# Half sums and differences of keys, and value products in two bursts: a change to a four-layer Trainium2 kernel

## The chip, the cores and the metric

One core of a Trainium2 chip runs the whole program. The metric is the device time of one execution in microseconds. The engines are TensorE (PE; PEld is its weight load), VectorE (DVE), ScalarE (ACT), GpSimd (POOL) and SyncE (SP), which here only issues DMAs.

## The reference, cut to what matters

Four transformer layers are applied in turn to x of 4 x 1024 x 128, each an attention and a feed-forward part, each added to x. The change lies in the attention of the first two layers, which have 16 heads of 8 features. Layer 1 is causal:

```python
scores = jnp.einsum('bthd,bshd->bhts', q, k) / math.sqrt(dk)
scores = jnp.where(causal_mask, -inf, scores)
attn = jax.nn.softmax(scores, axis=-1)
out = jnp.einsum('bhts,bshd->bthd', attn, v)
```

Layer 2 has no mask, has a bias on q, k and v, and subtracts the maximum of each row of scores in the open:

```python
scores = jnp.einsum('bhqd,bhkd->bhqk', q, k) * SCALE
scores = scores - jnp.max(scores, axis=-1, keepdims=True)
attn = jnp.exp(scores)
attn = attn / jnp.maximum(jnp.sum(attn, axis=-1, keepdims=True), 1e-12)
ctx = jnp.einsum('bhqk,bhkd->bhqd', attn, v)
```

## The kernel before

`project` normalises the rows, turns them and forms q, k and v in eight chunks of 512 rows. An item is q or k of one chunk: one fp32 product of 128x512 into `item_ps`, which is then split into three bf16 parts. ScalarE writes the first part (`high`), VectorE the remainder, ScalarE the second part (`middle`), GpSimd the third, and SP stores the three to DRAM. Its tensors are called p0 in layer 1 and p1 in layer 2; a page of the profile leaves such numbers out.

`narrow_attention` is used by both layers (tensors a0 and a1). A unit is one batch and four heads, 16 units in all. The bf16 parts of q and k lie as 6 pairs of 8 rows, 48 rows for a head; two heads share the 128 rows of an operand, one in each half, so that two products can lie in different rows of TensorE. Work of a unit comes in two kinds:

- Slots, for the row maxima. A slot is a product of 128 queries with 512 keys of one head, into one of three PSUM banks `slot_ps` (`a_slot`, L1181). VectorE reduces it to one column of `part_max` (L1344; in layer 1 with a mask added, L1340). There are 64 in a unit of layer 2: 4 heads, 8 tiles of 128 queries, 2 halves of the keys (`kh`). Layer 1 has 48, of 128 to 512 columns. A further slot takes the turn of the maxima (`max_turn`), and two that of the outputs (`o_turn`), which need the same banks. A bank is free again when `slot_done` says so.
- Steps, for the output: 16 of 128 keys by 512 queries (12 in layer 1, from 128 to 512 queries wide). In each, for e in 0, 1: two score products of two heads, transposed, with minus the maximum added through three further rows (L1203; masks L1210), and one exponential of ScalarE over both (L1321). Then the value products of the step before: four fp32 products of 32 columns each, for the four heads, into one bank `o_ps` (`values`, L1223). The last head's columns carry the sum of the exponentials along.

The slots run ahead: those for step n + 5 (layer 1: n + 6) are issued during step n (`ahead`), four a step in layer 2, so unit 0's and the first 20 of unit 1's come before the first step. TensorE's order is written out by hand: for each e a quarter of the step's slots, the two scores, another quarter; after both, the values. At the end of a half of the queries ScalarE copies `o_ps` out (`copy_out`, L1308), and the next half's first value product waits for that.

Of the kernel before, what the change touches and what calls it, by code (L numbers as in the profile page):

```python
# [7 lines left out]
BF16 = mybir.dt.bfloat16  # L8
# [109 lines left out]
def project(nc, name, src, mv, rstd, wq, wk, wv, qs, ks, vs, ident, load_early, gain=None, qk_bias=None, v_bias=None, fresh=None):  # L118


    NB, ITEMS = 4, 2
    groups = ((0,), (1,), (2, 3), (4, 5), (6, 7))
    with ExitStack() as ctx:
# [6 lines left out]
        def sem(n):  # L130
            return nc.alloc_semaphore(f"{name}_{n}")

        w_qk = [sb(f"w_qk{i}", [P, P]) for i in range(ITEMS)]
# [7 lines left out]
        gain_sb, bias_sb, vb_sb = sb("gain_sb", [P, 2]), sb("bias_sb", [P, ITEMS]), sb("vb_sb", [P, P])  # L141
# [5 lines left out]
                             "v_ready", "v_done"))  # L147
        stats_done, mv_done, std_done, root_step = (sem(n) for n in ("stats_done", "mv_done", "std_done", "root_step"))
        stored = [sem(f"stored{i}") for i in range(2 * NB)]
        v_stored = [sem(f"v_stored{i}") for i in range(4)]  # L150
        n_loads = 3 + sum(a is not None for a in (gain, qk_bias, v_bias))
# [3 lines left out]
        def _(sp):  # L155
# [4 lines left out]
            if qk_bias is not None:  # L160
                sp.dma_start(bias_sb[:], qk_bias).then_inc(loaded, 16)
            if v_bias is not None:
                sp.dma_start(vb_sb[:], v_bias.to_broadcast([P, P])).then_inc(loaded, 16)
            for c in range(CHUNKS):
                b, half = c // 2, c % 2
                for i in range(ITEMS):
                    n = c * ITEMS + i
                    sp.wait_ge(lo_done, n + 1)
                    sp.dma_start((qs, ks)[i][b, :, :, half * CH:(half + 1) * CH].rearrange("k f t -> f k t"),
                                 parts[n % (2 * NB)][:]).then_inc(stored[n % (2 * NB)], 16)  # L170
# [3 lines left out]
                if c == 3:  # L174
                    for i in range(4):
                        sp.wait_ge(stored[i], 16)
# [4 lines left out]
            for i in range(2 * NB):  # L181
                sp.wait_ge(stored[i], 16 * (CHUNKS * ITEMS // (2 * NB)))
# [4 lines left out]
        def _(te):  # L187
# [14 lines left out]
            for c in range(CHUNKS):  # L202
                te.wait_ge(xT_done, c + 1)
                for i in range(ITEMS):
                    n = c * ITEMS + i
                    if n >= NB:
                        te.wait_ge(rem_done, n - NB + 1)
                    nc.tensor.matmul(item_ps[n % NB][:], w_qk[i][:], xnT[c % 4][:], start=True, stop=True).then_inc(item_ready, 1)
# [10 lines left out]
        def _(act):  # L219
            def take(c):  # L220

                act.wait_ge(xT_ready, c + 1)
                if c >= 4:
                    act.wait_ge(v_ready, c - 3)
# [6 lines left out]
            def high(n):  # L231

                act.wait_ge(item_ready, n + 1)
                if n >= 2 * NB:
                    act.wait_ge(stored[n % (2 * NB)], n // (2 * NB) * 16)
                if qk_bias is None:
                    nc.scalar.activation(parts[n % (2 * NB)][:, 0, :], item_ps[n % NB][:], ACT.Copy).then_inc(hi_done, 1)
                else:
                    nc.scalar.activation(parts[n % (2 * NB)][:, 0, :], item_ps[n % NB][:], ACT.Identity,
# [2996 lines left out]
```

## Time and profile before

| | |
|---|---|
| median of 3 runs | 3596.66 us (3596.16 to 3596.76) |
| profiled execution | 3575.11 us, its span 3573.2 us |
| TensorE busy | 2981.4 us (83%) |
| VectorE busy | 2616.7 us (73%) |
| ScalarE busy | 2150.4 us (60%) |
| mean granted TensorE clock | 0.924 |

The busy shares are means over all stages. The steps of layer 1's attention run from about 111 to 553 us, those of layer 2's from 940 to 1594 us, with the projection of layer 2 before them, from about 838 us.

### The profile page before, as it was taken

How to read it: one execution, taken by the hardware profiler on the slowest of the kernel's cores; microseconds unless marked ns; L12 is line 12 of the kernel's file. 1: busy time of each engine (PE TensorE's matmuls, PEld its weight loads, DVE VectorE, ACT ScalarE, POOL GpSimd, SP SyncE). 2: the span in 40 equal slices, each digit the busy share in tenths (PEclk: the TensorE clock that was granted, in tenths of full speed). 3: DMA queues.
4: the chain of work that ended last, by engine and by line, in shares of the span. 5: the costliest groups of instructions: out<-in, count | busy, mean ns of one | idle time of the engine just before them, and what ended most of it. 6: DMA issues, size and time to landing. Idle time of an engine off the chain costs nothing. (4 is left out here: it accounts for less than half of the span.)

```text
span 3573.2 us, 51682 instructions
## 1 busy us (share of the span) xinstructions
PE 2981.4 (83%) x18320; PEld 1203.9 (34%) x18320; DVE 2616.7 (73%) x6042; ACT 2150.4 (60%) x2740; POOL 451.6 (13%) x633
## 2 busy tenths in 40 slices
PE   5999997896999999985799998967469988889836
PEld 2333333443122222223355555545322222222214
DVE  6999973666999999946566666640868888888821
ACT  2566673323377777773355555522369999899822
POOL 2000001333000000000000000014220011102023
PEclk7899998997799999997899999978779999999968
DMA  4443202343211111000000000011362222221102
GB/s 146 58 106 62 33 13 48 64 80 112 30 27 27 22 22 22 12 3 3 31 1 1 1 7 7 1 54 50 106 140 33 33 33 39 27 30 23 53 24 74
DMA packets 172975, 148.27 MB, mean 41 GB/s; under 512 B 79672, under 2 KB 130632, under 8 KB 172720
## 3 DMA queue, kind: packets, MB, share of 16 engines
q1 hardware_dynamic: 168624, 137.21, 19.2%
q0 software_dynamic: 4096, 7.78, 0.7%
q8 instruction: 145, 2.38, 0.3%
q14 instruction: 110, 0.90, 0.1%
HBM read 95.13 MB, written 49.68 MB: 41 GB/s over the span
## 5 line engine op out<-in xcount | busy, mean ns | idle before, releaser
L1321 ACT ACTIVATE a_probs<-a_scores 128x1024 f32<-128x1024 f32 (+3 forms) x896 | 791.5, 932 | 374.1 <-PE a_scores L1203 233.9
L1344 DVE TENSOR_REDUCE a_part_max<-a_slot_ps 128x1 f32<-128x512 f32 x1280 | 798.6, 684 | 30.9 <-PE a_slot_ps L1181 29.6
L2341 DVE TENSOR_TENSOR a_probs<-a_logit_ps,a_gate 128x1024 f32<-128x1024 f32 x512 | 602.4, 1219 | 98.8 <-ACT a_gate L2200 97.5
L1181 PE MATMUL a_slot_ps<-a_k_op,a_q_op 48*128 48x512 bf16 (+3 forms) x1792 | 579.1, 380 | 95.6 <-DMA a_mask_wide<-in_mask_wide 17.9
L2205 ACT ACTIVATE a_probs<-a_probs 128x2048 f32<-128x2048 f32 x256 | 488.1, 1907 | 7.7 <-DVE a_probs L2341 7.6
L1203 PE MATMUL a_scores<-a_q_op,a_k_op 51*128 51x512 bf16 (+3 forms) x1792 | 452.4, 361 | 7.1 <-ACT a_probs L1321 6.1
L1223 PE MATMUL a_o_ps<-a_probs,a_v_op 128*32 128x512 f32 (+3 forms) x3584 | 437.9, 561 | 1.2 <-ACT a_o_sb L1308 0.6
L1181 PEld LDWEIGHTS a_slot_ps<-a_k_op,a_q_op 48*128 48x128 bf16 x1792 | 150.2, 94 | 697.5 <-DVE a_part_max L1344 469.2
L2106 PE MATMUL a_logit_ps<-space 96*128 96x512 bf16 x1024 | 303.3, 387 | 71.2 <-DVE a_probs L2341 62.4
L2200 ACT ACTIVATE a_gate<-a_diff_ps 128x1024 f32<-128x1024 f32 x256 | 261.6, 1022 | 55.2 <-PE a_diff_ps L2106 47.5
L2119 PE MATMUL a_o_ps<-a_probs,a_v_op 128*32 128x512 f32 x2048 | 274.0, 607 | 7.0 <-DVE a_o_sb L2334 3.1
L1340 DVE CUSTOM_DVE_ANT_0 a_slot_ps<-a_slot_ps,a_mask_wide 128x128 f32<-128x128 f32 (+3 forms) x512 | 237.0, 516 | 5.1 <-PE a_slot_ps L1181 4.1
L757 ACT ACTIVATE a_turned_sb<-a_turn_ps 128x512 f32<-128x512 f32 x192 | 93.6, 488 | 208.0 <-PE a_turn_ps L632 207.8
L747 ACT ACTIVATE space<-space,a_lows 128x128 f32<-128x128 f32 (+7 forms) x256 | 195.2, 767 | 4.0 <-DVE a_lows L841 4.0
L632 PE MATMUL a_turn_ps<-ident_sb,space 128*128 128x128 f32 x1152 | 167.1, 277 | 22.7 <-DVE a_turned_sb L852 18.0
L852 DVE COPY a_turned_sb<-a_turn_ps 128x512 f32<-128x512 f32 x192 | 106.6, 555 | 95.6 <-PE a_turn_ps L632 95.1
L2106 PE MATMUL a_diff_ps<-space 96*128 96x512 bf16 x512 | 157.1, 389 | 15.1 <-DMA a_v_op<-scratch_v 15.1
L841 DVE CUSTOM_DVE_ANT_0 space<-a_score_ps,a_mask 128x512 f32<-128x512 f32 (+3 forms) x256 | 138.7, 587 | 37.3 <-PE a_score_ps L619 37.2
L2106 PEld LDWEIGHTS a_logit_ps<-space 96*128 96x128 bf16 x1024 | 77.0, 98 | 263.9 <-DVE a_probs L2341 219.4
L632 PEld LDWEIGHTS a_turn_ps<-ident_sb,space 128*128 128x128 f32 x1152 | 132.6, 141 | 70.1 <-issue 32.1
L619 PE MATMUL a_score_ps<-a_kT,a_qT 64*128 64x512 f32 (+3 forms) x768 | 152.3, 516 | 1.1 <-DVE a_lows L841 1.0
L646 PE MATMUL a_o_ps<-a_turned_sb,a_v 128*64 128x512 f32 (+3 forms) x768 | 149.9, 512 | 0.0
(400 smaller groups left out, 3758.3 us busy)
## 6 DMA issues: line engine op xcount, KB each, us to landing
e_coef<-coef_dram SPq DMA_DIRECT2D x16, 1024.0 KB, 9.9
a_q_op<-scratch_q SPq DMA_DIRECT2D x384, 32.0 KB
a_k_op<-scratch_k SPq DMA_DIRECT2D x384, 32.0 KB
scratch_q<-p_parts SPq DMA_DIRECT2D x24, 384.0 KB, 3.4
scratch_k<-p_parts SPq DMA_DIRECT2D x24, 384.0 KB, 3.4
space<-scratch_k SPq DMA_DIRECT2D x192, 32.0 KB
space<-scratch_g SPq DMA_DIRECT2D x192, 32.0 KB
space<-scratch_q SPq DMA_DIRECT2D x192, 32.0 KB
```

The costliest lines, as they stand in the source:

```text
L632: mm = nc.tensor.transpose(turn_ps[j][:, t * P:(t + 1) * P], rows_of(u, h, t)[0][:, j, kb * P:(kb + 1) * P], ident[:])
L1181: nc.tensor.matmul(out[:, 0:width], q_op[g][r0:r0 + MAX_ROW, e, qt * P:(qt + 1) * P], k_op[g][r0:r0 + MAX_ROW, e, kh * CH:kh * CH + width] ...
L1203: return nc.tensor.matmul(scores[e][:, jj, off:CH], k_op[g][r0:r1, e, kb * P:(kb + 1) * P], q_op[g][r0:r1, e, hq * CH + off:(hq + 1) * CH] ...
L1223: mm = nc.tensor.matmul(o_ps[32 * j:32 * (j + 1), off:CH], v_op[g][:, kb, 32 * j:32 * (j + 1)], probs[(u * S + n) % NB][:, j, off:CH], sta ...
L1321: nc.scalar.activation(probs[gs % NB][:, 2 * e:2 * e + 2, off:CH], scores[e][:, :, off:CH], ACT.Exp, scale=scale).then_inc(probs_done, 1)
L1340: nc.vector.tensor_tensor_reduce(out=slot[:, 0:w], in0=slot[:, 0:w], in1=mask_wide[:, CH - w:CH], scale=1.0, scalar=-3e38, op0=ALU.add, op ...
L1344: nc.vector.tensor_reduce(part_max[u % 2][:, kh, col:col + 1], slot[:, 0:w], axis=AX.X, op=ALU.max).then_inc(slot_done, 1)
L2106: mm = nc.tensor.matmul(out[:, j, :], ops[g][0][:, j, kb * P:(kb + 1) * P], q[:, j, hq * CH:(hq + 1) * CH], start=True, stop=True)
L2119: mm = nc.tensor.matmul(o_ps[c0:c0 + 32, :], v_op[g][:, kb, j * 32:(j + 1) * 32], probs[gs % 4][:, m, j, :], start=kb == 0, stop=kb == KB - 1)
L2200: nc.scalar.activation(gate[gs % 2][:], diff_ps[:], ACT.Tanh).then_inc(gate_done, 1)
L2205: nc.scalar.activation(tile[:], tile[:], ACT.Exp).then_inc(exp_done, 1)
L2341: nc.vector.tensor_tensor(probs[gs % 4][:, m, :, :], logit_ps[m][:], gate[gs % 2][:], op) \
```

## The change

In layer 2 only, the maximum over both halves of the keys is found for a quarter of the row tiles (those with an odd head of a pair and an odd query tile) by max(a, b) = (a + b) / 2 + |a - b| / 2. `project` forms a third kind of item, "h", once per batch: half sums and half differences of the two halves' keys, from weights that GpSimd halves (`w_half`), for one head of each pair. They go to `scratch_halves`, and SP loads them into `k_halves`. A slot with the differences (`apart`) goes to ScalarE, which writes its absolute value to `sizes`; VectorE skips it. The slot with the sums goes to VectorE, which adds `sizes` and takes the maximum in one instruction. The order of slots in a unit changes, and banks are freed by either of two semaphores. In both layers the value products of a step are issued in two bursts: after the slots and scores of e = 0 those of heads 0 and 1, after those of e = 1 those of heads 2 and 3.

```diff
@@ project, TensorE
+                    else:
+                        te.wait_ge(halved, 4)
+                        nc.tensor.matmul(item_ps[n % NB][:], w_half[0][:], xnT[(c - 1) % 4][:], start=True, stop=False)
+                        nc.tensor.matmul(item_ps[n % NB][:], w_half[1][:], xnT[c % 4][:], start=False, stop=True) \
+                            .then_inc(item_ready, 1)
...
@@ project, ScalarE
-                    act.wait_ge(v_ready, c - 3)
+                    act.wait_ge(v_ready, c - 2)
...
@@ project, GpSimd
+                for i, column, factor in ((0, 0, 0.5), (0, 1, 0.5), (1, 0, 0.5), (1, 1, -0.5)):
+                    nc.gpsimd.tensor_scalar(w_half[i][:].rearrange("p (g i e r) -> p g i e r", g=GROUPS, i=2, e=2)[:, :, column], odd,
+                                            factor, None, ALU.mult).then_inc(halved, 1)
...
@@ NarrowShape
+    EIGHT = ((0, 0, 0), (1, 0, 0), (0, 0, 1), (1, 1, 0), (0, 1, 0), (1, 0, 1), (0, 1, 1), (1, 1, 1))
...
+            self.slots = [(2 * e + jj, qt + odd, kh) for e in range(2) for qt in range(0, KB, 2) for jj, odd, kh in self.EIGHT]
...
+    def in_pair(self, s):
+        j, qt, kh = self.slots[s]
+        return not self.causal and j % 2 == 1 and qt % 2 == 1
+    def apart(self, s):
+        return self.in_pair(s) and self.slots[s][2] == 0
...
@@ NarrowOperands.load_qk, SP
+            if self.halves is not None:
+                src = self.halves[b, kp].rearrange("(g x r) t -> g r x t", g=GROUPS, r=8)
+                r0 = HALF_ROWS + n * 8
+                sp.dma_start(self.k_halves[g][r0:r0 + 8, :, :, :].rearrange("r i e t -> r (i e) t"), src[g]).then_inc(self.qk_loaded[g], 16)
...
@@ narrow_attention, TensorE
-                    te.wait_ge(slot_done, n - BANKS + 1)
+                    apart, count = shape.released[n - BANKS]
+                    te.wait_ge(size_done if apart else slot_done, count)
...
+                keys = k_op[g][r0:r0 + MAX_ROW, e, kh * CH:kh * CH + width]
+                if shape.in_pair(s):
+                    keys = operands.k_halves[g][r0:r0 + MAX_ROW, 1 - kh, e, :]
...
-            def values(u, n):
+            def values(u, n, e):
...
-                te.wait_ge(probs_done, (u * S + n + 1) * 2)
-                if n == 0:
+                te.wait_ge(probs_done, (u * S + n) * 2 + e + 1)
+                if n == 0 and e == 0:
                     te.wait_ge(v_spread, u + 1)
-                if kb == 0 and u * 2 + hq > 0:
+                if kb == 0 and e == 0 and u * 2 + hq > 0:
                     te.wait_ge(o_copied, u * 2 + hq)
-                for j in range(H):
+                for j in (2 * e, 2 * e + 1):
...
                         for v, s in todo[cut[2 * e + 1]:cut[2 * e + 2]]:
                             a_slot(v, s)
-                    if n > 0:
-                        values(u, n - 1)
-                    elif u > 0:
-                        values(u - 1, S - 1)
+                        if n > 0:
+                            values(u, n - 1, e)
+                        elif u > 0:
+                            values(u - 1, S - 1, e)
...
@@ narrow_attention, ScalarE
+            def slot_sizes(todo):
+                for u, s in todo:
+                    n = shape.place["slot", u, s]
+                    apart, count = shape.released[n]
+                    if apart:
+                        act.wait_ge(slot_ready, n + 1)
+                        if count > 2:
+                            act.wait_ge(slot_done, shape.released[shape.place["slot", *pairs[count - 3]]][1])
+                        nc.scalar.activation(sizes[(count - 1) % 2][:], slot_ps[n % BANKS][:], ACT.Abs).then_inc(size_done, 1)
...
                     for e in range(2):
+                        slot_sizes(todo[cut[2 * e]:cut[2 * e + 1]])
                         act.wait_ge(scores_ready, gs * 2 + e + 1)
...
                                              ACT.Exp, scale=scale).then_inc(probs_done, 1)
+                        slot_sizes(todo[cut[2 * e + 1]:cut[2 * e + 2]])
...
@@ narrow_attention, VectorE
+                if shape.apart(s):
+                    return
                 dve.wait_ge(slot_ready, n + 1)
+                if shape.in_pair(s):
+                    count = pairs.index((u, s)) + 1
+                    dve.wait_ge(size_done, count)
+                    nc.vector.tensor_tensor_reduce(out=slot[:], in0=slot[:], in1=sizes[(count - 1) % 2][:], scale=1.0,
+                                                   scalar=-3e38, op0=ALU.add, op1=ALU.max,
+                                                   accum_out=part_max[u % 2][:, kh, col:col + 1]).then_inc(slot_done, 1)
+                    return
```

On TensorE, from one step's value products to the next in the middle of layer 2's attention, the order of before is this (a row is line, operation, output and inputs, output's shape and the number in a row):

```order
L1223 MATMUL a1_o_ps<-a1_probs1,a1_v_op0 32x512 x4
L1181 MATMUL a1_slot_ps2<-a1_k_op2,a1_q_op2 128x512
L1203 MATMUL a1_scores0<-a1_q_op0,a1_k_op0 128x512 x2
L1181 MATMUL a1_slot_ps0<-a1_k_op2,a1_q_op2 128x512
L1181 MATMUL a1_slot_ps1<-a1_k_op2,a1_q_op2 128x512
L1203 MATMUL a1_scores1<-a1_q_op0,a1_k_op0 128x512 x2
L1181 MATMUL a1_slot_ps2<-a1_k_op2,a1_q_op2 128x512
L1223 MATMUL a1_o_ps<-a1_probs2,a1_v_op0 32x512 x4
```

The changed kernel has there:

```order
L1282 MATMUL a1_o_ps<-a1_probs3,a1_v_op1 32x512 x2
L1240 MATMUL a1_slot_ps0<-a1_k_op3,a1_q_op3 128x512
L1262 MATMUL a1_scores1<-a1_q_op2,a1_k_op2 128x512 x2
L1240 MATMUL a1_slot_ps1<-a1_k_halves3,a1_q_op3 128x512
L1282 MATMUL a1_o_ps<-a1_probs3,a1_v_op1 32x512 x2
L1240 MATMUL a1_slot_ps2<-a1_k_op3,a1_q_op3 128x512
L1262 MATMUL a1_scores0<-a1_q_op2,a1_k_op2 128x512 x2
L1240 MATMUL a1_slot_ps0<-a1_k_op3,a1_q_op3 128x512
L1282 MATMUL a1_o_ps<-a1_probs0,a1_v_op2 32x512 x2
```

The four value products of a step stand as two and two, with two slots and two scores ahead of each pair; the two slots that stood next to each other are parted by a pair.

On ScalarE, steps of the same stage before:

```order
L1321 ACTIVATE a1_probs0<-a1_scores1 128x1024
L1321 ACTIVATE a1_probs1<-a1_scores0 128x1024
L1321 ACTIVATE a1_probs1<-a1_scores1 128x1024
L1321 ACTIVATE a1_probs2<-a1_scores0 128x1024
L1321 ACTIVATE a1_probs2<-a1_scores1 128x1024
```

and in the changed kernel:

```order
L1398 ACTIVATE a1_probs0<-a1_scores0 128x1024
L1398 ACTIVATE a1_probs0<-a1_scores1 128x1024
L1398 ACTIVATE a1_probs1<-a1_scores0 128x1024
L1398 ACTIVATE a1_probs1<-a1_scores1 128x1024
L1380 ACTIVATE a1_sizes1<-a1_slot_ps1 128x512
L1398 ACTIVATE a1_probs2<-a1_scores0 128x1024
```

After every fourth exponential an absolute value of a difference slot has come in.

## Rows read from the trace of the kernel before

**Rows 1.** Busy time by stretch: attention of layer 1, attention of layer 2.

```profile
core 0: us, PE busy (x) PEld busy (x) DVE busy (x) ACT busy (x) POOL busy (x), PEclk, DMA share, GB/s
...
111.00:553.00 442.00, 412.32 (x4131) 162.13 (x4131) 374.71 (x1240) 303.88 (x412) 29.28 (x75) 1.00 0.29 54
940.00:1594.00 654.00, 620.67 (x4129) 133.52 (x4127) 605.98 (x1058) 508.77 (x541) 29.27 (x75) 1.00 0.14 20
...
```

**Rows 2.** Timeline of VectorE, start of attention in layer 2.

```profile
start us, us, engine line op out<-in xcount [idle before <-releaser]
...
885.17 38.36 DVE L1344 TENSOR_REDUCE a_part_max<-a_slot_ps 128x1 f32<-128x512 f32 x64 [14.56 <-PE a_slot_ps L1181]
...
```

**Rows 3.** Line of the row maxima: count, ns min/median/max, first and last start.

```profile
L1350 DVE TENSOR_TENSOR a_row_max<-a_part_max x4: 191/192/193, 207.8 to 293.2; 128x32 f32<-128x32 f32 x4
L1350 DVE TENSOR_TENSOR a_row_max<-a_part_max x4: 191/191/191, 1216.7 to 1342.5; 128x32 f32<-128x32 f32 x4
```

**Rows 4.** Timeline of TensorE, one step of attention in layer 2.

```profile
...
1226.34 1.07 PE L1223 MATMUL a_o_ps<-a_probs,a_v_op 128*32 128x512 f32 x8
1227.34 0.39 PE L1181 MATMUL a_slot_ps<-a_k_op,a_q_op 48*128 48x512 bf16 x1
1227.34 0.60 PE L1203 MATMUL a_scores<-a_q_op,a_k_op 51*128 51x512 bf16 x2
1227.57 0.64 PE L1181 MATMUL a_slot_ps<-a_k_op,a_q_op 48*128 48x512 bf16 x2
1228.51 0.39 PE L1181 MATMUL a_slot_ps<-a_k_op,a_q_op 48*128 48x512 bf16 x1
1228.82 1.06 PE L1223 MATMUL a_o_ps<-a_probs,a_v_op 128*32 128x512 f32 x8
...
```

**Rows 5.** Timeline of TensorE, attention in layer 1.

```profile
...
283.73 0.33 PE L1210 MATMUL a_scores<-a_mask_b,a_ident 64*128 64x128 bf16 x4
284.33 0.23 PE L1181 MATMUL a_slot_ps<-a_k_op,a_q_op 48*128 48x128 bf16 x1 [0.27 <-DVE a_part_max L1344]
284.48 0.85 PE L1223 MATMUL a_o_ps<-a_probs,a_v_op 128*32 128x384 f32 x8
285.26 0.66 PE L1195 MATMUL a_slot_ps<-ident_sb,a_o_sb 128*128 128x128 f32 x4
285.85 0.39 PE L1181 MATMUL a_slot_ps<-a_k_op,a_q_op 48*128 48x512 bf16 x1
...
```

**Rows 6.** Timeline of TensorE, attention of layer 3.

```profile
...
1900.48 1.94 PE L646 MATMUL a_o_ps<-a_turned_sb,a_v 128*64 128x512 f32 x8
1902.35 1.12 PE L666 MATMUL a_spare_ps<-a_xnT,a_w_q 128*128 128x512 f32 x2
```

**Rows 7.** Groups by shape, attention of layer 2: busy, mean ns, idle before.

```profile
...
L1344 DVE TENSOR_REDUCE a_part_max<-a_slot_ps 128x1 f32<-128x512 f32 x935 | 580.5, 683 | 1.9 <-PE a_slot_ps L1181 1.0
...
L1181 PEld LDWEIGHTS a_slot_ps<-a_k_op,a_q_op 48*128 48x128 bf16 x932 | 70.5, 93 | 397.3 <-DVE a_part_max L1344 356.7 <-DVE a_nat L1380 23.4 <-issue 14.1
...
L1308 ACT ACTIVATE a_o_sb<-a_o_ps 128x512 f32<-128x512 f32 x31 | 18.5, 598 | 1.2
...
```

**Rows 8.** Groups by shape, attention of layer 1.

```profile
...
L1340 DVE CUSTOM_DVE_ANT_0 a_slot_ps<-a_slot_ps,a_mask_wide 128x512 f32<-128x512 f32 x116 | 78.7, 719 | 0.0
...
L1181 PEld LDWEIGHTS a_slot_ps<-a_k_op,a_q_op 48*128 48x128 bf16 x688 | 62.6, 93 | 193.2 <-DVE a_part_max L1340 97.2 <-DVE a_part_max L1344 57.8 <-issue 22.8
...
```

**Rows 9.** Timeline of TensorE, a step without slots, layer 2.

```profile
...
1578.12 0.39 PE L1203 MATMUL a_scores<-a_q_op,a_k_op 51*128 51x512 bf16 x2 [0.20 <-ACT a_probs L1321]
1578.43 1.07 PE L1223 MATMUL a_o_ps<-a_probs,a_v_op 128*32 128x512 f32 x8
...
```

**Rows 10.** Timeline of ScalarE, the same stretch.

```profile
...
1573.30 6.59 ACT L1321 ACTIVATE a_probs<-a_scores 128x1024 f32<-128x1024 f32 x7
...
```

**Rows 11.** Timeline of TensorE, projection of layer 2.

```profile
...
857.24 1.88 PE L208 MATMUL p_item_ps<-p_xnT,p_w_qk 128*128 128x512 f32 x4
858.96 1.05 PE L212 MATMUL p_v_ps<-p_w_v,p_xnT 128*128 128x128 f32 x8
...
```

More of the change, by code:

```diff
@@ L114, in apply_norm, with project @@
     return ins
-def project(nc, name, src, mv, rstd, wq, wk, wv, qs, ks, vs, ident, load_early, gain=None, qk_bias=None, v_bias=None, fresh=None):
-    NB, ITEMS = 4, 2
+def project(nc, name, src, mv, rstd, wq, wk, wv, qs, ks, vs, ident, load_early, gain=None, qk_bias=None, v_bias=None, fresh=None, halves=None,
+            half_bias=None):
+    NB = 4
+    items = [(c, kind) for c in range(CHUNKS) for kind in ("qkh" if halves is not None and c % 2 else "qk")]
+    of_chunk = [[n for n, (c, _) in enumerate(items) if c == chunk] for chunk in range(CHUNKS)]
     groups = ((0,), (1,), (2, 3), (4, 5), (6, 7))
@@ L150, in project @@
         v_stored = [sem(f"v_stored{i}") for i in range(4)]
[L151 removed]
+        n_loads = 3 + sum(a is not None for a in (gain, qk_bias, v_bias, half_bias))
         block = ctx.enter_context(nc.Block())
@@ L1005, in __init__ @@
         self.n = len(self.steps)
-        self.place = {}
+        self.place, self.released = {}, []
+        count = {False: 0, True: 0}
         for key in self.slot_order():
             self.place[key] = len(self.place)
+            apart = key[0] == "slot" and self.apart(key[2])
+            count[apart] += 1
+            self.released.append((apart, count[apart]))
+    def in_pair(self, s):
[3 more added lines that the diff above has]
+        return self.in_pair(s) and self.slots[s][2] == 0
     def off(self, hq, kb):
@@ L1059, in __init__ @@
         self.v_loaded = [nc.alloc_semaphore(f"{name}_v_loaded{i}") for i in range(GROUPS)]
-        self.qs, self.ks, self.vs = qs, ks, vs
+        self.qs, self.ks, self.vs, self.halves = qs, ks, vs, halves
+        self.loads = 4 * len(PAIR_PARTS)
+        if halves is not None:
+            self.k_halves = [sb(f"k_halves{i}", [P, 2, 2, CH], BF16) for i in range(GROUPS)]
+            self.loads += len(PAIR_PARTS)
     def load_qk(self, sp, u, parts=range(len(PAIR_PARTS))):
@@ L1120, in narrow_attention @@
         block = ctx.enter_context(nc.Block())
-        N_QK, N_MAX = 4 * len(PAIR_PARTS), 6
+        N_QK, N_MAX = operands.loads, 6
+        pairs = [key[1:] for key in shape.place if key[0] == "slot" and shape.in_pair(key[2]) and not shape.apart(key[2])]
         def column_of(j, qt):
@@ L1267, in _ @@
                         max_turn(u + 1)
-            values(UNITS - 1, S - 1)
+            for e in range(2):
+                values(UNITS - 1, S - 1, e)
             o_turn(UNITS - 1, 1)
@@ L1312, in _ @@
                     off, gs = shape.off(hq, kb), u * S + n
+                    todo = shape.ahead(u, n)
+                    cut = [len(todo) * p // 4 for p in range(5)]
                     if n == 1 and u > 0:
```

99 lines of the change are left out of this document (61 added, 38 removed).

## The prediction

> **What bounds the kernel now.** I read first the busy time by stretch, for the two stages that hold the change: attention of layer 1 (causal, "a0") and of layer 2 ("a1") [rows 1]. In a1 VectorE is busy 605.98 us of 654, TensorE 620.67. Both look full, so shares don't decide; the timeline does. Before the score steps begin, VectorE takes its 64 row maxima alone in 38.36 us, 0.60 each [rows 2]. The instruction that ends a unit's maxima comes 4 times between 1216.7 and 1342.5, so a unit takes 41.93 us [rows 3], of which 64 x 0.60 = 38.4 is that work. TensorE's weight loads for slots wait 356.7 us for VectorE [rows 7]. So VectorE sets a1's pace, through the three slot banks.
>
> Next, how much room TensorE has. In one step of a1 [rows 4] the four value products start together at 1226.34 (x8, since an fp32 product is two passes) and the next matmul starts at 1227.34: 1.00 us. Then come a slot with a score (both at 1227.34, in different halves of the rows), a pair 0.23 later, a slot with a score again, a score, a slot by itself that waited for a bank (1228.51), and 0.31 after it the value products again. Of the step's 2.48 us TensorE needs 1.00 + 4 x 0.23 + 0.31 = 2.23. It has 0.25 us of room.
>
> In a0 the pieces are narrower [rows 5]: value products 384 wide hold TensorE from 284.48 to 285.26, 0.78, so 0.22 less per 128 columns: 0.57 at 256 and 0.36 at 128, by estimate. A unit takes (293.2 - 207.8) / 3 = 28.47 us [rows 3]. TensorE's gaps there: its busy column leaves 442 - 412.32 = 30 us over 15.5 units [rows 1], 1.9 a unit, too few because ends are modelled; the slots' weight loads waited 97.2 + 57.8 = 155 us for VectorE [rows 8], 10 a unit, too many because matmuls still ran meanwhile. Counted in starts, four mask matmuls from 283.73, 0.06 apart, and a slot at 284.33 leave about 0.37 in that step [rows 5], 4.4 for 12 steps. I take 4.4 and keep both ends.
>
> **The change, part by part.**
>
> *Value products in two bursts (both stages).* A step's four products over four column groups become two and two, with scores and two slots between. The question is what two cost. The third layer's attention has it: two products of 64 columns each, two passes, and the same again, from 1900.48 to 1902.35, 1.87 us, so 0.93 for a group of two [rows 6]. Four together took 1.00. Two cost as much as four: splitting adds one whole burst a step. (The Trainium skill, "TensorE: Matmul & The Clock Gate", Part 3, measured speedup vs the span model, speaks against the change too: a packed group spans one matmul plus about 4 ns for each further tile. By that a pair saves under 0.02 us and the sum below stays.)
>
> a1: a half step becomes slot with score, 0.23, score with slot, 0.31, two products, 1.00: 1.54 us. A step is 3.08, a unit 16 x 3.08 = 49.3. To it come two output turns of 0.59 (four transposes, 285.26 to 285.85) [rows 5], the turn of the maxima, about 0.2, and a new wait: the first burst of a new half of the queries starts 1.54 after the last burst of the old one, but ScalarE must first copy the sums out: burst 1.07 [rows 4], copy 0.60 [rows 7], about 0.1 of signals, 1.77, so 0.23 late, twice a unit. Together 51.2 against 41.93: +9.3 a unit. Units 0 to 13 and 11 of 16 steps of unit 14 carry slots: 14.7 x 9.3 = +136. The last 21 steps carry none; ScalarE paces them now, 7 exponentials in 6.59 us [rows 10], 0.93 each, with copies 1.92 a step. After, a half is a pair of scores, 0.31 later the burst [rows 9], and 1.00: 2.62 a step, 21 x 0.70 = +15.
>
> a0: the added bursts of a unit are six of 512 (1.00 each) and two each of 384, 256 and 128: 6.0 + 1.6 + 1.1 + 0.7 = 9.4. Going into a burst costs about 0.09 more than going on (0.31 against 0.23), 1.1 a unit. Less the room of 4.4: +6.1, over 14.5 units with slots +89. The last 18 steps have no slots: an added 10.5 / 12 = 0.88, less an idle of 0.38 as in a1's tail (1.92 less 1.00 + 0.23 + 0.31), +9.
>
> *Half sums and differences (a1 only).* Of a unit's 64 slots 16 use half keys: eight differences, whose absolute value ScalarE takes, and eight sums, which VectorE adds to them and reduces. VectorE loses 8 x 0.60 = 4.8 us a unit and pays, for each of eight, 0.04 more at the same size (719 ns [rows 8] against 683 [rows 7]) and at worst 0.14 for the accumulator's read: -4.5 at best, -3.4 at worst. It then needs 37.4 of a unit of 51: **none of it reaches the end** while TensorE paces; what hides it is the added burst. Without that it would be worth 14.7 x 4.5 = 66 us. ScalarE gets eight absolute values, each like the 512-wide copy: 32 x 0.93 + 10 x 0.60 = 35.8 of 51, hidden. A difference slot holds its bank until the exponential ahead and its own turn are through, 0.4 + 0.93 + 0.6 = 1.9 us; the bank is wanted three slots on, 0.31 + 1.00 + 1.54 = 2.8 later. Hidden, with 0.9 to spare. TensorE's count of slots stays. Before the steps VectorE has 10 slots fewer of 84, -6.
>
> *Projection of layer 2.* Four more items of two fp32 products of 512; two such hold TensorE from 857.24 to 858.96, 1.72 us [rows 11], and the next work follows at once: 4 x 1.72 = +7. Six more loads a unit on SP lie beside 50 us of other work, four small GpSimd products before its first item. The changed wait for an earlier chunk's values costs nothing: TensorE has passed there before the item that ScalarE takes first.
>
> Sum: layer 2 +136 + 15 - 6 + 7 = +152, layer 1 +89 + 9 = +98, together **+250**. The profiled execution took 3575.11 us (span 3573.2) and would take 3825. The median of the runs, 3596.66, is 21.6 higher: **3847**.
>
> **Rivals.**
>
> *A pair costs half of four; faster.* Products on 32 columns might leave sooner than those on 64. At 0.50 a half step of a1 is 1.04, TensorE 2.1 a step, and VectorE paces with 37.4: -66 - 6 + 7. In a0 half the bursts' cost, 4.7 + 1.1 - 4.4 = 1.4 a unit, +20. Total 3552. It turns at a burst of about 0.63: a1 then (0.54 + 0.63) x 32 + 1.9 = 39.3 a unit, -38, and a0 +38. Against it: a pass takes 0.47 us in the groups of two, 0.50 in a group of four by itself and 0.43 where one product fills the array [rows 4, 6, 11]. The same mechanism at 0.63 is also the way to no change, 3597.
>
> *Bursts overlap their neighbours.* If two products on half the columns ran beside the next slots, a half step would be 0.23 + 0.23 + 0.93 = 1.39: a1 +4.4 a unit, +65 and +8 at the tail, a0 at half, +45: 3716. For it: slots and scores do start together [rows 4]. Against: those lie in different rows, while value products take all 128 rows and slots all 128 columns. (The Trainium skill, "TensorEngine Tiling (Array Packing)", Key Properties, lets tiles run independently, which is this rival, but also drains the array at each change of mode, which is the forecast; the trace, with 1.00 alone and 0.93 in a row, sides with the drain.)
>
> *The absolute values come late.* Behind exponentials and copies, each of 128 could hold its bank 1.3 longer than allowed for, 0.4 past its need: +50, 3897.
>
> **How the numbers follow.** Forecast 0.80, late absolute values 0.08, overlap 0.07, half price 0.03, the 0.63 between 0.02. The terms' bounds: a0's room of 1.9 or 10 gives +36 or -81; a1's half step down to 1.39 gives -71; late absolute values +50. They don't all meet: 3770 to 3905 leaves out overlap, half price, no change, and part of the forecast's own tails, 2 in 10. The kernel's three runs lie within 0.6 us; 0.2%, 7 us, is about the least that can be told from no change. Faster 0.03, same 0.02, slower 0.95.
>
> **What the profile will show.** If right: in a1 a step near 3.1 us, a unit near 51, TensorE starting without gaps, VectorE waiting for slots, its busy share falling from 93% to some 66%; in a0 a unit near 34.6; value products in groups of x4 with about 1.00 to the next start. Wrong, if pairs are followed within 0.7 us, if slots' weight loads still wait for VectorE or for the absolute values, or if a0's unit hardly moves, which would put its room near 10.

## The result, and the profile after

The changed kernel takes 3853.31 us (median of 4 runs, 3849.26 to 3855.27), the kernel before 3596.41 (4 runs, 3595.97 to 3596.76): 1.0714 times as long, interval 1.0701 to 1.0728, +256.9 us. The forecast was 3847, range 3770 to 3905. The profiled execution took 3852.48 us, with a span of 3850.7. It lies at its median, while before's profiled one lies 21 below its own. So the two traces differ by 277 us, and some 20 of them lie behind layer 2's attention, in code that the change leaves alone; below only the stages that it touches are compared.

Busy time by stretch of the changed kernel, attention of layer 1 and of layer 2, against [rows 1]:

```profile
110.00:653.00 543.00, 519.30 (x4137) 178.84 (x4135) 388.54 (x1244) 319.13 (x414) 29.24 (x75) 1.00 0.24 44
1047.00:1852.00 805.00, 796.73 (x4138) 147.48 (x4139) 564.77 (x1059) 594.56 (x659) 29.23 (x75) 1.00 0.16 20
```

In layer 2 TensorE is now busy 797 of 805 us and VectorE 565, which is 70%; it was 93%. The granted clock reads 1.00 in both stretches, as before, so it has no part in this.

The line that ends a unit's row maxima, in layer 2 and then in layer 1 (count, ns min/median/max, first and last start):

```profile
L1437 DVE TENSOR_TENSOR a_row_max<-a_part_max x6: 191/193/193, 1335.3 to 1590.2; 128x32 f32<-128x32 f32 x6
L1437 DVE TENSOR_TENSOR a_row_max<-a_part_max x4: 192/192/193, 228.4 to 331.8; 128x32 f32<-128x32 f32 x4
```

Six of them lie five units apart: 254.9 / 5 = 50.98 us a unit in layer 2, where [rows 3] gave 41.93, and 103.4 / 3 = 34.47 in layer 1, where they gave 28.47.

TensorE's timeline of the changed kernel, two half steps of layer 2, against [rows 4]:

```profile
1399.77 1.05 PE L1282 MATMUL a_o_ps<-a_probs,a_v_op 128*32 128x512 f32 x4
1400.76 0.39 PE L1240 MATMUL a_slot_ps<-a_k_op,a_q_op 48*128 48x512 bf16 x1
1400.76 0.60 PE L1262 MATMUL a_scores<-a_q_op,a_k_op 51*128 51x512 bf16 x2
1400.98 0.38 PE L1240 MATMUL a_slot_ps<-a_k_halves,a_q_op 48*128 48x512 bf16 x1
1401.29 1.05 PE L1282 MATMUL a_o_ps<-a_probs,a_v_op 128*32 128x512 f32 x4
...
1404.34 1.05 PE L1282 MATMUL a_o_ps<-a_probs,a_v_op 128*32 128x512 f32 x4
...
1406.18 1.05 PE L1282 MATMUL a_o_ps<-a_probs,a_v_op 128*32 128x512 f32 x4 [0.25 <-ACT a_o_sb L1369]
```

Read the starts: a burst of two value products (x4, two passes each) at 1399.77, the next work 0.99 later. It cost 1.00 when it had four products. The half step, burst to burst, is 1.52 us, the step 3.04, and no matmul in it waits. In [rows 4] the step was 2.48. The last row is a half step that begins a new half of the queries: it waits 0.25 for ScalarE's copy of the finished sums (`a_o_sb`) and comes 1.84 after the burst before it.

The costliest groups of the changed kernel in layer 2, by shape (busy, mean ns, idle before and its releaser), against [rows 7]:

```profile
L1240 PE MATMUL a_slot_ps<-a_k_op,a_q_op 48*128 48x512 bf16 x701 | 235.5, 385 | 0.0
...
L1431 DVE TENSOR_REDUCE a_part_max<-a_slot_ps 128x1 f32<-128x512 f32 x702 | 460.6, 687 | 164.1 <-PE a_slot_ps L1240 163.5
...
L1422 DVE CUSTOM_DVE_ANT_0 a_slot_ps<-a_slot_ps,a_sizes 128x512 f32<-128x512 f32 x117 | 80.7, 690 | 0.0
...
L1380 ACT ACTIVATE a_sizes<-a_slot_ps 128x512 f32<-128x512 f32 x117 | 69.3, 592 | 0.0
...
L1240 PEld LDWEIGHTS a_slot_ps<-a_k_op,a_q_op 48*128 48x128 bf16 x700 | 49.1, 93 | 369.4 <-DVE a_part_max L1431 256.6 <-ACT a_sizes L1380 90.6 <-issue 20.6
```

VectorE now waits 164 us for slots, where it waited 1.9. The last row is one to read with care: the slots' weight loads still show 256.6 us "for VectorE" and 90.6 for the absolute values. But the slots' matmuls, in the first row, show no idle time (0.0), and in the timeline above they start as soon as the burst is through. A weight load also stands idle while a burst keeps TensorE busy, and the releaser named is only the signal that came last. The matmuls' starts decide, not the loads' idle time.

One wait of the slots is real, once a unit, in the half step with the turn of the maxima. Rows of three engines:

```profile
1337.66 1.05 PE L1282 MATMUL a_o_ps<-a_probs,a_v_op 128*32 128x512 f32 x4
...
1338.69 0.59 ACT L1380 ACTIVATE a_sizes<-a_slot_ps 128x512 f32<-128x512 f32 x1
...
1339.33 0.09 PEld L1240 LDWEIGHTS a_slot_ps<-a_k_op,a_q_op 48*128 48x128 bf16 x1 [0.36 <-ACT a_sizes L1380]
...
1339.65 1.05 PE L1282 MATMUL a_o_ps<-a_probs,a_v_op 128*32 128x512 f32 x4
```

The absolute value ends at 1339.28 and gives its bank back, the half step's second slot is loaded at 1339.33, and the burst follows 0.32 later, 1.99 after the one before it. In the kernel with the bursts alone (the first experiment) the same half step takes 1.74, so a late absolute value costs 0.25 us a unit.

### The profile page after: what moved, and what is told of

The parts are those of the page before. It is cut to its first block and busy times, and to the rows that moved or that the text cites. A ratio compares the mean times of both kernels' runs of the same rounds, so it can differ in the third digit from the quotient of the medians.

```text
span 3850.7 us, 52232 instructions
## 1 busy us (share of the span) xinstructions
PE 3277.4 (85%) x18336; PEld 1242.6 (32%) x18336; DVE 2588.2 (67%) x6048; ACT 2261.9 (59%) x2876; POOL 457.5 (12%) x641
## 5 line engine op out<-in xcount | busy, mean ns | idle before, releaser
L1398 ACT ACTIVATE a_probs<-a_scores 128x1024 f32<-128x1024 f32 (+3 forms) x896 | 833.3, 932 | 474.9 <-PE a_scores L1262 278.2
L1282 PE MATMUL a_o_ps<-a_probs,a_v_op 128*32 128x512 f32 (+3 forms) x3584 | 862.5, 560 | 29.5 <-ACT a_o_sb L1369 29.4
L1431 DVE TENSOR_REDUCE a_part_max<-a_slot_ps 128x1 f32<-128x512 f32 x1024 | 666.8, 686 | 197.5 <-PE a_slot_ps L1240 194.3
L2428 DVE TENSOR_TENSOR a_probs<-a_logit_ps,a_gate 128x1024 f32<-128x1024 f32 x512 | 602.3, 1219 | 103.4 <-ACT a_gate L2287 99.8
L1240 PE MATMUL a_slot_ps<-a_k_op,a_q_op 48*128 48x512 bf16 (+3 forms) x1536 | 501.6, 375 | 42.4 <-PEq L126 16.8
L1262 PE MATMUL a_scores<-a_q_op,a_k_op 51*128 51x512 bf16 (+3 forms) x1792 | 485.3, 362 | 0.5 <-ACT a_probs L1398 0.4
L1240 PEld LDWEIGHTS a_slot_ps<-a_k_op,a_q_op 48*128 48x128 bf16 x1536 | 123.2, 94 | 678.9 <-DVE a_part_max L1431 353.8
L1282 PEld LDWEIGHTS a_o_ps<-a_probs,a_v_op 128*32 128x32 f32 x3584 | 130.7, 108 | 302.4 <-ACT a_probs L1398 218.9
L1350 POOL TENSOR_TENSOR a_max_parts<-a_neg_max,a_zeros 32x128 bf16<-32x128 f32 x32 | 12.4, 388 | 1271.2 <-DVE a_neg_max L1446 1271.2
```

The lines of the kernel that those rows point to most:

```text
L1240: nc.tensor.matmul(out[:, 0:width], q_op[g][r0:r0 + MAX_ROW, e, qt * P:(qt + 1) * P], keys, start=True, stop=True).then_inc(slot_ready, 1)
L1262: return nc.tensor.matmul(scores[e][:, jj, off:CH], k_op[g][r0:r1, e, kb * P:(kb + 1) * P], q_op[g][r0:r1, e, hq * CH + off:(hq + 1) * CH] ...
L1282: mm = nc.tensor.matmul(o_ps[32 * j:32 * (j + 1), off:CH], v_op[g][:, kb, 32 * j:32 * (j + 1)], probs[(u * S + n) % NB][:, j, off:CH], sta ...
L1398: nc.scalar.activation(probs[gs % NB][:, 2 * e:2 * e + 2, off:CH], scores[e][:, :, off:CH], ACT.Exp, scale=scale).then_inc(probs_done, 1)
L1431: nc.vector.tensor_reduce(part_max[u % 2][:, kh, col:col + 1], slot[:, 0:w], axis=AX.X, op=ALU.max).then_inc(slot_done, 1)
L2428: nc.vector.tensor_tensor(probs[gs % 4][:, m, :, :], logit_ps[m][:], gate[gs % 2][:], op) \
```

## The experiments

Each kernel is compared with runs of the kernel before on its own chip: 3582.53 us in the first four, 3595.86 in the next three, 3596.15 in the last two. The chips differ by 13 us for the same kernel, so only ratios and differences on one chip are used. "Unit" is the distance of two row maxima, as above.

### The two bursts alone

The kernel before, with its value products split as in the change, and no half keys:

```diff
-            def values(u, n):
+            def values(u, n, e):
...
-                te.wait_ge(probs_done, (u * S + n + 1) * 2)
+                te.wait_ge(probs_done, (u * S + n) * 2 + e + 1)
...
-                for j in range(H):
+                for j in (2 * e, 2 * e + 1):
...
-                    if n > 0:
-                        values(u, n - 1)
+                        if n > 0:
+                            values(u, n - 1, e)
```

> The kernel before with only the value products in two bursts, in both layers; no half keys. Theory (each step pays one more burst of about 1.0 us on TensorE, and TensorE then paces both stages, so that the half keys are hidden): as the changed kernel less its longer projection and plus its shorter start, a unit of layer 2 at 51.0 us, of layer 1 at 34.5, time 3596 + 151 + 98 - 7 = 3845 to 3852. Rival (part of the loss comes from ScalarE's absolute values and the banks they hold): a unit of layer 2 clearly under 51, the time under 3830. Second rival (the half keys give back some of the loss even beside the bursts): time over 3865.

Measured: 3826.14 us, 1.0683 (1.0665 to 1.0701), +243.6. Its row maxima in layer 2 are five units apart here:

```profile
L1352 DVE TENSOR_TENSOR a_row_max<-a_part_max x6: 191/192/193, 1324.3 to 1578.0; 128x32 f32<-128x32 f32 x6
```

A unit is 253.7 / 5 = 50.74 us, 0.24 short of the changed kernel's, and layer 1's is 34.47, the same. The 0.24 is the late absolute value shown above. The bursts alone make 244 of the 257 us, a little less than the 249 to 256 expected. The rest, 13, is of the size of what the half keys add: the longer projection and the stretch behind it (+8), 15 units of 0.25 (+4), less a shorter start (-3: from the first slot to the first value product is 54.7 us here and 51.4 in the changed kernel). These come to 9, within what the two intervals allow.

### The half keys alone

The changed kernel, with four products in one burst at the end of a step, as before:

```diff
-                for j in (2 * e, 2 * e + 1):
+                for j in range(H):
...
-                        if n > 0:
-                            values(u, n - 1, e)
+                    if n > 0:
+                        values(u, n - 1)
```

> The changed kernel with the four value products in one burst after both exponentials, as before; half keys stay. Theory: layer 1 back to 28.5 us a unit; in layer 2 VectorE needs about 37.4 us a unit and TensorE about 16 x 2.23 + 1.4 = 37.1, so a unit at 38, time 3596 - 14.7 x 3.9 - 6 + 7 = 3540, between 3530 and 3550. Rival (the absolute values hold their banks too long when TensorE is not slowed): a unit at 40 or more, time 3565 to 3600, slots' weight loads waiting for the absolute values.

Measured: 3587.63 us, 1.0018 (1.0006 to 1.0029), +5, where -46 to -66 was expected. Nothing was gained, and a unit stayed at 41.92. That is the sign that the expectation gave its rival, absolute values that hold their banks too long, so both have to be looked at. First the busy time of 500 us of layer 2, of the kernel before:

```profile
1000.00:1500.00 500.00, 476.37 (x3161) 102.68 (x3161) 493.44 (x860) 382.98 (x406) 23.42 (x60) 1.00 0.14 22
```

and of this kernel:

```profile
1000.00:1500.00 500.00, 484.77 (x3163) 103.08 (x3155) 438.58 (x859) 429.58 (x502) 23.41 (x60) 1.00 0.20 27
```

VectorE did fall from 493 to 439 busy us, 11%. Yet as many matmuls ran, 3163 against 3161. Its timeline, rows of several engines, shows why:

```profile
1219.30 1.06 PE L1282 MATMUL a_o_ps<-a_probs,a_v_op 128*32 128x512 f32 x8
...
1220.30 0.39 PE L1240 MATMUL a_slot_ps<-a_k_op,a_q_op 48*128 48x512 bf16 x1
...
1220.72 1.89 DVE L1429 TENSOR_REDUCE a_part_max<-a_slot_ps 128x1 f32<-128x512 f32 x3 [0.60 <-PE a_slot_ps L1240]
1220.93 0.09 PEld L1240 LDWEIGHTS a_slot_ps<-a_k_op,a_q_op 48*128 48x128 bf16 x1 [0.52 <-ACT a_sizes L1378]
...
1221.47 0.39 PE L1240 MATMUL a_slot_ps<-a_k_halves,a_q_op 48*128 48x512 bf16 x1
1221.79 0.16 PEld L1282 LDWEIGHTS a_o_ps<-a_probs,a_v_op 128*32 128x32 f32 x8 [0.23 <-issue]
```

VectorE stands idle 0.60 us until the burst is over and a slot comes. The first slot starts at 1220.30 and its maximum at 1220.72; that maximum takes 0.69, to 1221.41. The fourth slot of the step, the second row from below, starts at 1221.47: with three banks it needs the first slot's. 0.32 after it the next burst may start. Burst 1.00 + 0.42 + 0.69 + 0.06 + 0.32 = 2.49 us, the whole step. So the new theory: layer 2 is paced by a ring (a burst, the first slot, its maximum, the fourth slot in the same bank, the next burst), and not by the sum of VectorE's work, though in the kernel before VectorE was busy 98.7% of these 500 us. That share overstates it: a maximum's record lasts 0.68 us, but maxima in a row start 0.60 apart [rows 2], so four take 2.40 of the 2.49.

The row shows also why the half keys could not help. The slot with half keys is the fourth of a step, in every step of these 500 us, whether it holds differences or sums. The first slot's maximum, the one in the ring, is a plain one with and without them. A slot did wait for an absolute value, the third (1220.93), but the fourth would not have started earlier for it, and the steps took 2.49 as before. An order with a difference slot first was not tried.

### Bursts in one layer only

The kernel before, split in layer 1 and with one burst in layer 2:

```diff
+                        if shape.causal:
+                            if n > 0:
+                                values(u, n - 1, e)
...
+                    if not shape.causal:
+                        if n > 0:
+                            values_all(u, n - 1)
```

> The kernel before with two bursts in layer 1 only. Theory: + 98 us, 3695, a unit of layer 1 at 34.5 us and layer 2 as before at 41.93. With the bursts alone in both layers this gives layer 2's share, + 151, by difference. Rival (layer 1's cost in the trace was partly something else): under 3680 or over 3710.

Measured: 3684.48 us, 1.0284 (1.0266 to 1.0301), +102, against 98 in the sum. Layer 2's share is the rest of the first experiment: 243.6 - 102 = 142, with no half keys, where 151 was expected; each of the two differences is good to some 6 us.

### One product and three

The changed kernel, its bursts of unequal size:

```diff
-                for j in (2 * e, 2 * e + 1):
+                for j in ((0,), (1, 2, 3))[e]:
```

> The changed kernel with its bursts split as one product (head 0) and three (heads 1 to 3) instead of two and two. Theory (a burst costs the passes of one product whatever its number): the same time as the changed kernel within 5 us, 3853. Rival (a product's price is its own, so a burst of three costs more and one of one less, and the sum is uneven): each burst's distance to the next start differs, 0.75 and 1.25 us, and where VectorE paces the short half the time changes by over 10 us.

Measured: 3838.63 us, 1.0723 (1.0704 to 1.0743), +256, as the changed kernel. TensorE's timeline of it:

```profile
1401.44 1.06 PE L1282 MATMUL a_o_ps<-a_probs,a_v_op 128*32 128x512 f32 x6
1402.43 0.39 PE L1240 MATMUL a_slot_ps<-a_k_op,a_q_op 48*128 48x512 bf16 x1
...
1402.97 1.05 PE L1282 MATMUL a_o_ps<-a_probs,a_v_op 128*32 128x512 f32 x2
1403.95 0.39 PE L1240 MATMUL a_slot_ps<-a_k_op,a_q_op 48*128 48x512 bf16 x1
```

Three products (x6) hold TensorE 0.99 us, one (x2) holds it 0.98, or 0.95 in the few bursts that come behind a wait for the copied sums. As medians over 500 us of layer 2, one product holds TensorE 0.978, two (the changed kernel) 0.985, three 0.991 and four (the kernel before) 0.998. So a burst costs its two passes and some 7 ns for each further product. (The Trainium skill, "TensorE: Matmul & The Clock Gate", Part 3, measured speedup vs the span model, gives a packed group one matmul's time and about 4 ns for each further tile; these medians agree in kind, with 7 ns in its place.)

### One burst in the middle of a step

If the ring closes around the burst, a burst elsewhere might open it. The kernel before, with all four products of the step two back issued after the first pair of heads, and the copy of finished sums moved with it; then the same edit on the changed kernel:

```diff
-                    if n > 0:
-                        values(u, n - 1)
-                    elif u > 0:
-                        values(u - 1, S - 1)
+                        if e == 0 and gs >= 2:
+                            values(*divmod(gs - 2, S))
...
+            values(UNITS - 1, S - 2)
             values(UNITS - 1, S - 1)
```

> The kernel before, without half keys; the four value products stay one burst, but it stands between the slots and scores of e = 0 and those of e = 1, for the step two back, in both layers (the copy of the sums moves to between the two exponentials). Theory now (layer 2's step of before, 2.486 us, is a ring of latencies: the fourth slot of a step waits for the bank of the first, 0.42 to be seen + 0.69 reduced + 0.06, then 0.32 to the value products and 1.00 for them; parting the slots two and two opens the ring): VectorE's own 64 x 0.60 + 2.2 paces, a unit at 40.5, - 21 us in layer 2, and a like gain in layer 1, in all - 20 to - 50 against before. Rival (VectorE's throughput paced before): no change, a unit at 41.9. Second rival (the exponentials' wait for the later products costs more): slower.

> The changed kernel with the same one burst in the middle, for the step two back: half keys and an open ring. Theory of the ring: VectorE 33.9 + 2.2 and ScalarE 35.8 us a unit, TensorE 16 x 2.0 + 1.4, so a unit of layer 2 near 37.5, - 65 in layer 2, + 5 for projection and start, with layer 1's gain - 80 to - 100 against before. Rival (the ring isn't what held the halves back, ScalarE's absolute values are): a unit over 40, no better than the kernel without half keys.

Measured, without half keys: 3573.08 us, 0.9937 (0.9923 to 0.9951), -22.8. It is the fastest of the kernels that leave no work out. Measured, with half keys: 3586.72, 0.9978 (0.9969 to 0.9987), -9, where -80 to -100 was expected. The row maxima of the kernel without half keys, layer 2 and layer 1:

```profile
L1349 DVE TENSOR_TENSOR a_row_max<-a_part_max x4: 193/193/193, 1201.3 to 1326.7; 128x32 f32<-128x32 f32 x4
L1349 DVE TENSOR_TENSOR a_row_max<-a_part_max x13: 191/193/193, 176.6 to 504.5; 128x32 f32<-128x32 f32 x13
```

Layer 1's first row maximum shown here and its last are twelve units apart: 327.9 / 12 = 27.33 us, against 28.48 before. From the first value product of layer 1 to the last it took 422.8 us, before 441.5: 18.7 of the 23 us. The same in layer 2 is 650.4 against 653.7; its unit is 125.4 / 3 = 41.8, as before, and 42.15 with half keys. The hope for layer 2 fell both times. That -22.8 lies within the expected -20 to -50 is luck: 21 of it were to come from layer 2, which gave 3. A step of the one with half keys:

```profile
1221.70 1.06 PE L1282 MATMUL a_o_ps<-a_probs,a_v_op 128*32 128x512 f32 x8
1222.69 0.39 PE L1240 MATMUL a_slot_ps<-a_k_op,a_q_op 48*128 48x512 bf16 x1
...
1222.92 0.38 PE L1240 MATMUL a_slot_ps<-a_k_halves,a_q_op 48*128 48x512 bf16 x1
1223.14 0.38 PE L1240 MATMUL a_slot_ps<-a_k_op,a_q_op 48*128 48x512 bf16 x1
...
1223.87 0.39 PE L1240 MATMUL a_slot_ps<-a_k_op,a_q_op 48*128 48x512 bf16 x1
```

Wherever the burst stands, four slots stand between it and the next, so the fourth still waits for the first one's bank: 1223.87 - 1222.69 = 1.18 us. The half keys are now the second slot, again not the first. Moving the burst turned the ring and did not open it. The kernel with half keys did meet the sign of its rival, a unit over 40 and no better than without them. But the kernel without half keys has no absolute values and kept the step of 2.49 too, so they aren't what holds it. The unit is 0.33 us longer with half keys (42.15 against 41.82), all of it in the steps with a turn of the outputs or of the maxima; whether late absolute values make it was not followed up.

### Two bursts side by side

The changed kernel, both bursts with their own waits, but issued one behind the other at the end of the step:

```diff
                         for v, s in todo[cut[2 * e + 1]:cut[2 * e + 2]]:
                             a_slot(v, s)
+                    for e in range(2):
                         if n > 0:
                             values(u, n - 1, e)
```

> The changed kernel with both bursts issued after e = 1, next to each other, each with its own wait. Theory (a burst costs because it stands apart on TensorE, not because it is waited for twice): the same time as the half keys with one burst, within 5 us of before. Rival (the second wait or the break between the two costs): + 100 us or more.

Measured: 3604.45 us, 1.0022 (1.0013 to 1.0031), +8.6. That is outside the 5 us that were expected, but the interval (+5 to +11) meets that of the half keys alone (+2 to +10), and a unit is 41.94. Its burst in TensorE's timeline:

```profile
1203.99 1.06 PE L1282 MATMUL a_o_ps<-a_probs,a_v_op 128*32 128x512 f32 x8
1204.99 0.39 PE L1240 MATMUL a_slot_ps<-a_k_op,a_q_op 48*128 48x512 bf16 x1
```

The two join into one burst of 1.00 (x8). The second wait costs nothing that shows, the number of products next to nothing; the 250 us come from the two bursts standing apart, with other work between.

### A shorter maximum, in the ring and beside it

This is the test of the ring. In the kernel before, VectorE reads only 256 of the 512 columns of one slot in each step of layer 2: the first slot of the step in one kernel, the third in the other. The left-out columns are work left out, so these are no versions to use. VectorE saves nearly the same in both, 0.26 and 0.27 us a step.

```diff
                 else:
+                    if not shape.causal and s % 4 == 0:
+                        w = w // 2
```

(with `s % 4 == 2` in the second kernel)

> The kernel before; in layer 2 VectorE reduces only 256 of the 512 columns of the first slot of each step (so a quarter of the row tiles' maxima miss columns: work left out). That takes 0.27 us off VectorE's work in each step and off the wait of the fourth slot for the first one's bank. Ring theory: step from 2.487 to 2.22, stopped by TensorE's 2.23: a unit near 38, - 55 us, and - 6 before the first step. Throughput theory: VectorE 4 x 0.60 - 0.27 = 2.12 a step, the same gain.

> The same with the third slot of each step cut to 256 columns in place of the first (work left out in the same measure). Ring theory: the fourth slot still waits for the first one's bank, 1.17 us, so the step stays at 2.487, a unit at 41.9; only the start gains, - 6 us. Throughput theory (what the prediction took for layer 2 before): the same gain as with the first slot, - 55 to - 60.

Measured, first slot short: 3527.33 us, 0.98 (0.9784 to 0.9816), -69, where -61 was expected. Third slot short: 3591.9, 0.9982 (0.9973 to 0.9992), -4, where the ring asked for -6 and VectorE's total for -55 to -60. The maximum of 256 columns with the first slot short, its row maxima, and TensorE's starts:

```profile
L1346 DVE TENSOR_REDUCE a_part_max<-a_slot_ps 128x1 f32<-128x256 f32 x207 | 87.6, 423 | 1.0
```

```profile
L1352 DVE TENSOR_TENSOR a_row_max<-a_part_max x8: 191/192/193, 1223.6 to 1487.2; 128x32 f32<-128x32 f32 x8
```

```profile
1202.23 0.39 PE L1181 MATMUL a_slot_ps<-a_k_op,a_q_op 48*128 48x512 bf16 x1
...
1203.14 0.39 PE L1181 MATMUL a_slot_ps<-a_k_op,a_q_op 48*128 48x512 bf16 x1
```

and with the third slot short:

```profile
L1346 DVE TENSOR_REDUCE a_part_max<-a_slot_ps 128x1 f32<-128x256 f32 x191 | 79.1, 414 | 0.0
```

```profile
1201.32 0.39 PE L1181 MATMUL a_slot_ps<-a_k_op,a_q_op 48*128 48x512 bf16 x1
...
1202.49 0.39 PE L1181 MATMUL a_slot_ps<-a_k_op,a_q_op 48*128 48x512 bf16 x1
```

Look at first to fourth slot. It is 1203.14 - 1202.23 = 0.91 us with the first maximum short, and 1202.49 - 1201.32 = 1.17 with the third: that is what it is in [rows 4], 1228.51 - 1227.34 = 1.17. The 0.26 us taken from the first maximum came off the step whole: a step is now 2.22 us and a unit 263.6 / 7 = 37.66. The same 0.26 or so, taken from the third, came off nothing. If VectorE's total had set the pace, both would have gained alike. The 2.22 is also what TensorE needs for a step's own work, 2.23 by the prediction's sum, so whether a still shorter first maximum would gain more isn't shown.

## Why the prediction was right, and where a step of it was not

**A burst of two costs as much as four.** Right, and shown three ways: 0.99 us for two in the timeline, +244 us with the bursts alone, and 0.98 to 1.00 for one, two, three and four products. Half price and overlap with the neighbours both fell: the next slot starts 0.98 or more after a burst does, whatever the burst holds. The prediction had 0.93 from groups of two products of 64 columns in layer 3 and put 1.00, the price of four, into the sum; 0.985 was measured. That a change of mode drains the array, which the prediction drew on, no run measures by itself; they show that a burst and its neighbours don't overlap.

**Layer 2's steps, +136, and its end, +15.** A half step of 1.54 measured 1.52. A unit of 51.2 measured 50.98. The wait for the copied sums at a new half of the queries was put at 0.23 late and measured 0.32: 1.84 - 1.52. A half step with an output turn was 2.11, so 0.59 for the turn, as taken. The turn of the maxima took 0.22 (1.74 - 1.52, bursts alone), as taken, but brought the 0.25 of a late absolute value, which the sum put at nothing. That the unit still comes out so near is partly luck: half steps shorter by 0.02, 32 times, stand against 0.18 and 0.25 too little. From the first value product to the last of the stage is 653.7 us before and 804.6 after, +150.9, where 151 was forecast. In the steps without slots, TensorE's timeline of the changed kernel shows the half of 2.62 / 2 = 1.31 that the sum took, against [rows 9]:

```profile
1835.81 1.05 PE L1282 MATMUL a_o_ps<-a_probs,a_v_op 128*32 128x512 f32 x4
1836.80 0.39 PE L1262 MATMUL a_scores<-a_q_op,a_k_op 51*128 51x512 bf16 x2
1837.12 1.05 PE L1282 MATMUL a_o_ps<-a_probs,a_v_op 128*32 128x512 f32 x4
```

**Layer 1, +89 and +9.** The room of 4.4 us a unit was chosen between 1.9 and 10, and came out: the unit was put at 34.6 and measured 34.47. It was one step's gap, counted twelve times, so the closeness owes something to luck. The end of the layer, put at +9, was put too low: from the last slot to the last value product it went from 33.7 to 47.2 us, +13.5. The stage grew from 441.5 to 543.1 us, +101.6, and with the burst in layer 1 alone the kernel grew by 102.

**Projection, +7, and start, -6.** The four more items took 1.71 us each; the timeline of the changed kernel, against [rows 11]:

```profile
953.45 1.02 PE L223 MATMUL p_item_ps<-p_xnT,p_w_half 128*128 128x512 f32 x2
954.31 1.02 PE L224 MATMUL p_item_ps<-p_xnT,p_w_half 128*128 128x512 f32 x2
955.16 1.05 PE L229 MATMUL p_v_ps<-p_w_v,p_xnT 128*128 128x128 f32 x8
```

The stage, from the first rows normalised to VectorE's last remainder, went from 33.11 to 39.87, +6.8, and 1.6 more passed before attention began, which no term had. From the first slot to the first value product is 55.9 before and 51.4 after, -4.5. The half keys make 3.6 of that (52.3 with them alone), where the sum took 6 for ten slots fewer. All together: 101.6 + 150.9 + 6.8 + 1.6 - 4.5 = 256.4. Two stretches are not in it: the start of layer 1's attention, 1.4 shorter (41.65 to 40.28), and the stretch between that attention and layer 2's projection, 2.8 longer in these two traces, which no part of the change explains. With them it is 257.8, beside 256.9 between the medians.

**"VectorE sets a1's pace, through the three slot banks", and "Without that it would be worth 14.7 x 4.5 = 66 us".** This is the step that failed. The forecast took VectorE's total, 64 x 0.60 = 38.4 of 41.93 us, for the limit, and took from it the worth of lighter work; it left the other 3.5 us without a cause. "Through the three slot banks" was right, the total was not: with the half keys alone VectorE lost 11% of its work, a unit stayed at 41.92, and the time rose by 5 us instead of falling by 46 to 66. The two short maxima showed the cause: 0.26 us a step off the first gave 69 us, off the third 4. The claim cost the forecast nothing, since with the bursts apart TensorE paces either way: its own work in a step is 3.04 us, more than the ring's 2.49. It ruined the forecast of the half keys alone. The rival "half price", too, rested on VectorE's total for its 3552; that price was never met, so its number wasn't tried.

**VectorE's costs.** The combined operation on a slot of sums takes 690 ns and the plain maximum 687, so adding the absolute values costs 3 ns, where 40 were taken. Its accumulator is read in a further 142 ns. Whether that delays the next maximum, a question of 0.14 us in the forecast, VectorE's timeline of the kernel with half keys and the burst in the middle shows, at a place where the next slot was ready:

```profile
1223.73 0.69 DVE L1419 CUSTOM_DVE_ANT_0 a_slot_ps<-a_slot_ps,a_sizes 128x512 f32<-128x512 f32 x1
1224.33 0.14 DVE L1419 DVE_READ_ACCUMULATOR2_ANT a_part_max<- 128x1 f32 x1
1224.33 1.97 DVE L1428 TENSOR_REDUCE a_part_max<-a_slot_ps 128x1 f32<-128x512 f32 x3
```

The next maximum starts 0.60 after the combined operation, as after a plain one, and at the same time as the read: it delays nothing. VectorE's share was put at 66% and is 70%.

**Absolute values late.** In the changed kernel they are late once a unit, by the 0.25 us shown above, some 4 us in all, where the rival had 50 and the forecast nothing. In the kernel with the half keys alone the slots' loads waited for them in 500 us for 39.9, beside 119.9 for the maxima, but its steps took the 2.49 of the kernel before. What they would cost once the ring is open was not tried.

**The signs.** One sign of being wrong was "if slots' weight loads still wait for VectorE or for the absolute values". To the letter it came, 256.6 and 90.6 us, though the forecast held. It was a bad sign, since the loads' idle time doesn't tell whether a matmul started late. The matmuls' starts were the better sign, and the prediction named them too.

What is left open is why the stretch between the two layers' parts grew by 2.8 us, and how much of layer 1's gain with the burst in the middle (-1.15 us a unit) comes from the burst's place and how much from the copy moved with it; the two were moved together.

## What to carry to other kernels

A group of matmuls packed side by side on TensorE, as measured here with fp32 products of 32 columns, is bought by its passes, not by its members: before splitting one for an earlier start, multiply the whole burst by the number of parts that stand apart. And an engine busy 98.7% of a stage isn't yet the limit: follow the buffers round once, from the wait that ends last to the work that frees its bank, and add up the ring. If the ring's sum is the step, lighter work helps only where it lies in the ring, and there it helps in full until the next limit; moving the burst within the step turned the ring here without shortening it. So look which slot of the step the lighter work falls on before writing it: here it was never the first.

## What the runs showed of the hardware

One fp32 value product on 32 of the 128 columns, 512 wide, holds TensorE 0.98 us in its surroundings, two 0.985, three 0.99, four beside each other 1.00. The same two passes cost 0.86 where one fp32 product fills the array and the like follows it (953.45 to 954.31 above). How much of the difference is the change from one kind of matmul to the other wasn't measured by itself. VectorE's maximum of 512 columns out of PSUM takes 680 to 687 ns, of 256 columns 414 to 423, so some 145 to 166 ns of it don't depend on the width, by estimate from the two widths in the kernels with a short maximum; in a row such maxima start 600 ns apart. The read of an accumulator behind it, 142 ns, doesn't delay the next one. ScalarE's absolute value of 512 columns takes 592 ns. A unit kept its length within 0.01 us, 41.93 to 41.92, while an engine lost a ninth of its work.
